# The slots' bias as a one-row product in TensorE, and the last low-rank additions dealt to VectorE and GpSimd in turn

## What is computed

```python
query = hidden_states @ Wq.T
rq = query @ Wr.T
rk = aux_keys @ Wr.T
router_scores = jnp.einsum('bsr,nr->bsn', rq, rk) / np.sqrt(RDIM) + log_rel
top_scores, top_idx = jax.lax.top_k(router_scores, K)
sel_keys = aux_keys[top_idx]
attn = jnp.einsum('bsd,bskd->bsk', query, sel_keys) / np.sqrt(BOT) + log_rel[top_idx]
w = jax.nn.softmax(attn, axis=-1)
...
aux_out = aux_out @ Wvd.T @ Wvu.T
...
gate = jax.nn.sigmoid(gate_w1 * u_norm + gate_bias)
...
return hidden_states + gate[..., None] * aux_out
```

## Time and profile before

| | us |
|---|---|
| median of 3 runs | 1425.62 (1423.89 to 1426.12) |
| the profiled execution | 1426.41 |
| its span, first to last instruction | 1423.6 |
| PE busy | 1351.8 (95%) |
| DVE busy | 1177.8 (83%) |
| ACT busy | 953.3 (67%) |
| POOL busy | 704.9 (50%) |

### The profile page before, as it was taken

One profiled execution on the slowest core, in us unless ns is written; L12 is line 12 of the kernel. 1 busy time (PEld: TensorE's weight loads), 2 busy tenths in 40 slices (PEclk: granted clock), 3 DMA queues, 4 the chain that ended last, 5 costly groups with the idle time before them and its releaser, 6 DMA issues.

```text
span 1423.6 us, 25847 instructions
## 1 busy us (share of the span) xinstructions
PE 1351.8 (95%) x8474; PEld 754.3 (53%) x8604; DVE 1177.8 (83%) x2877; ACT 953.3 (67%) x2463; POOL 704.9 (50%) x596
## 2 busy tenths in 40 slices
PE   4779999998999999999999999999999999999995
PEld 3444555554455555555555555555555555555553
DVE  7887978889899887988878898889777798778657
ACT  5568777676677676667667667667666676666754
POOL 3376767677765344445545454435543454434321
PEclk8899999999999999999999999999999999999998
DMA  8466766787777566656567655657666677556443
GB/s 281 164 137 136 199 184 174 186 190 176 179 167 167 109 146 147 138 126 146 140 127 165 134 132 141 127 127 161 135 138 124 141 147 160 113 136 134 93 89 119
DMA packets 439828, 211.20 MB, mean 148 GB/s; under 512 B 382016, under 2 KB 383344, under 8 KB 439696
## 3 DMA queue, kind: packets, MB, share of 16 engines
q1 hardware_dynamic: 438144, 208.18, 63.6%
q10 hardware_dynamic: 1552, 1.38, 0.3%
HBM read 91.00 MB, written 25.17 MB: 82 GB/s over the span
## 4 chain that ended last, share of the span: by engine, by line
PE 70%; DVE 15%; ACT 5%; issue 4%; POOL 4%; DMA 1%; DVEq 0%; SPq 0%; ACTq 0%
PE PJ L1536 16%; PE PJ L1537 15%; PE PJ L1535 15%; DVE phl L1256 4%; PE PV L1708 4%; PE PV L1703 4%; PE PV L1704 4%; PE SC L1724 4%; PE SC L1722 4%; PE SC L1723 4%; POOL t L629 2%; ACT p L839 2%; DVE p L1246 2%; DVE t L1202 2%; DVE t L1200 1%
## 5 line engine op out<-in xcount | busy, mean ns | idle before, releaser
L651 POOL TENSOR_TENSOR oTl<-of,oTf 128x512 f16<-128x512 f32 x128 | 154.1, 1204 | 437.3 <-ACT oTf L831 437.1
L839 ACT ACTIVATE p<-p,mn 128x512 f32<-128x512 f32 (+3 forms) x512 | 280.9, 550 | 96.6 <-DVE mn L1246 96.5
L1256 DVE SCALAR_TENSOR_TENSOR phl<-p,ri,phl 128x128 f16<-128x128 f32 (+3 forms) x512 | 329.3, 683 | 0.0
L850 ACT ACTIVATE phl<-p,ri 128x128 f16<-128x128 f32 (+3 forms) x512 | 245.6, 550 | 4.1
L1535 PE MATMUL PJ<-XT,wsp 128*128 128x512 f16 x628 | 238.9, 380 | 4.0 <-DVE t L1202 3.9
L629 POOL TENSOR_TENSOR t<-t 128x512 f32<-128x512 f32 x158 | 201.7, 1277 | 77.3 <-DVE t L1202 76.8
L1536 PE MATMUL PJ<-XT,wsp 128*128 128x512 f16 x628 | 238.8, 380 | 0.0
L1537 PE MATMUL PJ<-XT,wsp 128*128 128x512 f16 x628 | 238.5, 380 | 0.0
L1246 DVE CUSTOM_DVE_ANT_0 p<-SC,maskw 128x512 f32<-128x512 f32 (+3 forms) x512 | 219.8, 485 | 2.1
L1536 PE MATMUL PJ<-wosp,oTf 128*128 128x512 f16 x512 | 194.0, 379 | 4.3
L634 POOL TENSOR_TENSOR qTl<-t,qTh 128x512 f16<-128x512 f32 x127 | 148.5, 1170 | 92.5 <-ACT qTh L815 92.5
(11 more groups left out here) (263 smaller groups left out, 2589.6 us busy)
## 6 DMA issues: line engine op xcount, KB each, us to landing
wsp<-kept SPq DMA_DIRECT2D x146, 256.0 KB, 3.0
wosp<-kept SPq DMA_DIRECT2D x96, 256.0 KB, 3.2
raw<-in_wqkv SPq DMA_DIRECT2D x48, 256.0 KB, 3.5
kept<-wsp SPq DMA_DIRECT2D x42, 256.0 KB, 2.5
raw<-in_wo SPq DMA_DIRECT2D x32, 256.0 KB, 4.4
kept<-wosp SPq DMA_DIRECT2D x32, 256.0 KB, 3.0
pTf<-phl SPq DMA_TRANSPOSE x256, 3.8
X<-in_x SPq DMA_DIRECT2D x3, 1024.0 KB, 9.8
```

The lines of the kernel that those rows point to most:

```text
L839: ins = nc.scalar.activation(pt, pt, ACT.Exp, bias=mn[:, par, i:i + 1], scale=-1.0, accum_out=rs[:, par, i:i + 1])
L850: nc.scalar.activation(phl[:, par, high(i, 0):high(i, i) + 1:3, :], p[:, par, SOFF[i]:SOFF[i] + w].rearrange("p (k t) -> p k t", t=P), ACT ...
L1256: nc.vector.scalar_tensor_tensor(out=phl[:, par, low(i, 0):low(i, i) + 1, :], in0=p[:, par, SOFF[i]:SOFF[i] + w].rearrange("p (k t) -> p k ...
```

## The change

For the two batches that are done apart (the first FFN's first, the second FFN's last), the bias goes into PSUM by PE: a product with one row (`ones[0:1]` by `lr2`, f32, 256 columns) starts each of the four score tiles, and the three 16-bit products add to it. `lr2` holds the bias and its negative. The factors go into `bh` and `bl` when they are made (`fqb`). `take_scores` is left out there, and `top` reads the scores from PSUM. In the other batches `take_scores` stays, with a plain addition.

`query_factors` in the head gets two factors more and, behind a wait for `ld_fs`, the two instructions that fill `lr2`.

At the end tiles 7, 9 and 11 go the way of 1, 3 and 5: scaled by ACT, added by POOL. POOL's first addition waits until the last selection is done (`r_mn[1]`). DVE's additions 0 and 2 stand behind `inverse_sums`, 4 and 6 behind `e_lo`. The products are made in the order 5, 7, 4, ET, 6, 8, 9, 11, 10, 12 to 15. The variance of tiles 14 and 15 is made behind the norming of tile 12 and ahead of that of tile 13.

```diff
-        + [(("AUX", 1, 1, n - 4), n) for n in (4, 5, 6)] + [(("ET", 1, 3, 0), 1)]
-        + [(("AUX", 1, n // 4, n % 4), k) for n, k in ((7, 7), (8, 3), (9, 0), (10, 2), (11, 4), (12, 5), (13, 6), (14, 7),
-                                                       (15, 3))])
+        + [(("AUX", 1, n // 4, n % 4), k) for n, k in ((5, 5), (7, 7), (4, 4))] + [(("ET", 1, 3, 0), 1)]
+        + [(("AUX", 1, n // 4, n % 4), k) for n, k in ((6, 6), (8, 0), (9, 3), (11, 5), (10, 2), (12, 4), (13, 7), (14, 6),
+                                                       (15, 0))])
...
-        odd = [1, 3, 5]
+        odd = [1, 3, 5, 7, 9, 11]
...
+            pool.wait_ge(r_mn[1], NT)
             for n in odd:
                 aux_add(n)
...
             exps_ffn(1, bb, (3,))
+            aux_odd(5)
             tail_sigmoid(10, 12, NT)
             e_hi(1, bb)
-            aux_odd(5)
+            aux_odd(7)
             tail_sigmoid(11, 12, NT)
             base(2, bb, 3)
+            aux_odd(9)
+            aux_odd(11)
...
-                nc.vector.scalar_tensor_tensor(out=rsc[:, ts, :], in0=both[:, :, 0:NSLOT], scalar=RDIM ** -0.5, in1=lr,
-                                               op0=ALU.mult, op1=ALU.add)
...
+                nc.vector.tensor_tensor(rsc[:, ts, :], both[:, :, 0:NSLOT], lr, ALU.add)
...
             def top(f, bb, tiles):
-                dve.wait_ge(r_use[f], 4 * bb + tiles[-1] + 1)
+                if apart(f, bb):
+                    dve.wait_ge(r_sc[f], 4 * bb + tiles[-1] + 1)
+                    if bb:
+                        dve.wait_ge(r_t[f], 4 * bb)
+                    route = {i: score_bank(f, bb, i)[:, 0:NSLOT] for i in tiles}
+                    attn = {i: score_bank(f, bb, i)[:, NSLOT:2 * NSLOT] for i in tiles}
...
                 nc.vector.reciprocal(fqr[:, :], fqs[:, :]).then_inc(fs_dve, 1)
+                nc.vector.tensor_scalar(fqb[:, 0:1], fqs[:, :], RDIM ** -0.5, None, ALU.mult)
+                nc.vector.tensor_scalar(fqb[:, 1:2], fqs[:, :], -BOT ** -0.5, None, ALU.mult).then_inc(fs_dve, 1)
+                dve.wait_ge(ld_fs, 96)
+                nc.vector.tensor_copy(lr2[0:1, 0:NSLOT], lrb[0:1, :])
+                nc.vector.tensor_scalar(lr2[0:1, NSLOT:2 * NSLOT], lrb[0:1, :], -1.0, None, ALU.mult).then_inc(fs_dve, 1)
...
             def select_first(i):
-                take_scores(0, 0, (i,))
                 top(0, 0, (i,))
...
             normal(2, bb, 0)
+            variance_of_squares(2, 4)
             normal(2, bb, 1)
-            variance_of_squares(2, 4)
...
             def select(*tiles):
-                take_scores(1, bb, tiles)
                 top(1, bb, tiles)
...
-            add(0)
-            add(2)
             learned(1, bb)
             gate_1(1, 12, NT, 4)
             inverse_sums(1, 12, NT, 4)
-            add(4)
-            add(6)
+            add(0)
+            add(2)
             dve.wait_ge(g_exd, 11)
             gate_2(1, 12, NT)
             e_lo(1, bb)
-            add(7)
+            add(4)
+            add(6)
             dve.wait_ge(g_exd, 12)
             gate_3(12, NT)
             scales(1, 12, NT)
-            for n in range(8, NT):
+            add(8)
+            add(10)
+            for n in range(12, NT):
                 add(n)
...
+                    if apart(f, bb):
+                        mm(dst, ones[0:1, :], lr2[:, :], start=True, stop=False)
+                    mm3(dst, qfh[:, ts], qfl[:, ts], bh[:, :], bl[:, :], not apart(f, bb), True).then_inc(r_sc[f], 1)
```

More of the change, by code:

```diff
@@ L145 @@
 PREPARED = {"pe": ["rk", "rmat", "wqT", "u1T", "v2"], "act": ["rk", "wq sums", "wq rows", "wq", "b0", "b1", "wu1", "v2"],
-            "dve": ["wq scales", "wq", "b0", "b1", "u1T", "v2"]}
+            "dve": ["wq scales", "b scales", "lr2", "wq", "b0", "b1", "u1T", "v2"]}
 def prepared(engine, what):
@@ L249, in macaron_kernel @@
         fql, fqs, fqr = (sb(n, [P, 1], F32) for n in ("fql", "fqs", "fqr"))
+        fqb = sb("fqb", [P, 2], F32)
+        lr2 = sb("lr2", [1, 2 * NSLOT], F32)
         fwvdT = sb("fwvdT", [P, CC, VB], F32)
@@ L356, in rope_index, with product @@
             return 5 * n if kind == "K" else 5 * n + idx + 1
-        odd = [1, 3, 5]
+        odd = [1, 3, 5, 7, 9, 11]
+        PRODUCTS = [4 * t[2] + t[3] for t, _ in TAIL if t[0] == "AUX"]
+        def product(f, n):
+            return PRODUCTS.index(n) + 1 if f else n + 1
         def odd_tile(f, n):
@@ L888, in _ @@
             act.wait_ge(fs_pe, prepared("pe", "rmat"))
-            nc.scalar.activation(bh[:, 0:NSLOT], SC[:, 1, 0:NSLOT], ACT.Copy, scale=fqs[:, 0:1]).then_inc(fs_act, 1)
-            nc.scalar.activation(bh[:, NSLOT:2 * NSLOT], fkeyT[:, :], ACT.Copy, scale=fqs[:, 0:1]).then_inc(fs_act, 1)
+            act.wait_ge(fs_dve, prepared("dve", "b scales"))
+            nc.scalar.activation(bh[:, 0:NSLOT], SC[:, 1, 0:NSLOT], ACT.Copy, scale=fqb[:, 0:1]).then_inc(fs_act, 1)
+            nc.scalar.activation(bh[:, NSLOT:2 * NSLOT], fkeyT[:, :], ACT.Copy, scale=fqb[:, 1:2]).then_inc(fs_act, 1)
             act.wait_ge(ld_fu, 16)
@@ L983, in aux_odd @@
             def aux_odd(n):
-                act.wait_ge(r_aux[1], n + 1)
+                act.wait_ge(r_aux[1], product(1, n))
                 act.wait_ge(r_gs[1], 1 if n < 12 else 2)
@@ L1079, in take_scores @@
                 i0, i1 = tiles[0], tiles[-1] + 1
-                if len(tiles) == 2:
-                    both = bank(("SCR", f, bb, i0 // 2)).rearrange("p (t n) -> p t n", t=2)
-                else:
-                    both = score_bank(f, bb, i0).unsqueeze(1)
+                both = bank(("SCR", f, bb, i0 // 2)).rearrange("p (t n) -> p t n", t=2)
                 lr = lrb[:, :].unsqueeze(1).to_broadcast([P, i1 - i0, NSLOT])
@@ L1101, in top @@
             def top(f, bb, tiles):
-                dve.wait_ge(r_use[f], 4 * bb + tiles[-1] + 1)
+                if apart(f, bb):
[4 more added lines that the diff above has]
+                    attn = {i: score_bank(f, bb, i)[:, NSLOT:2 * NSLOT] for i in tiles}
+                else:
+                    dve.wait_ge(r_use[f], taken(f, bb) + tiles[-1] + 1)
+                    route = {i: rsc[:, i, :] for i in tiles}
+                    attn = {i: asc[:, f, i, :] for i in tiles}
                 for i in tiles:
-                    ins = nc.vector.max(m8[:, i, :], rsc[:, i, :])
+                    ins = nc.vector.max(m8[:, i, :], route[i])
                 link(ins)
                 for i in tiles:
-                    ins = nc.vector.match_replace(mr[:, i, :], m8[:, i, :], rsc[:, i, :], SELECTED)
+                    ins = nc.vector.match_replace(mr[:, i, :], m8[:, i, :], route[i], SELECTED)
                 link(ins)
@@ L1182, in aux_add @@
                 n = 4 * bb + i
-                dve.wait_ge(r_aux[f], n + 1)
+                dve.wait_ge(r_aux[f], product(f, n))
                 dve.wait_ge(x_up[2 * f], n + 1)
```

20 lines of the change are left out of this document (11 added, 9 removed).

## The result

The changed kernel takes 1434.0 us (median of 6 runs, 1432.04 to 1434.97) against 1425.87 us for the kernel before in the same session: a ratio of 1.0057, 95% interval 1.0046 to 1.0068. It is 8.1 us slower. The forecast was 1427.1, and its range ended at 1429.6: the sign was right, the size was not. The profiled execution has a span of 1433.2 us, 9.6 more than before (the two executions themselves, 1434.97 and 1426.41, are 8.56 apart; 1 us of the difference lies outside the spans).

A forecast was written before the change was run, and what follows sets the result against it. PE's chain (70% of the span) was taken to bound the kernel, the output's stores its end. Head +1.7 and end -0.2 gave +1.5 on the median 1425.62: 1427.1 us, range 1424.4 to 1429.6.

The forecast's parts named there:

- The clock in the head and at the end: Head: clock rises when it did, giving back 0.8 us of the query's 1.5 delay; end: low-clock cost kept as before.
- PE stays at its lower clock in the head: Rival, head: PE's standstill during DVE's wait delays the clock's rise, 2.5 us more, 1429.6 us; chance 0.17.
- The one-row product: Both stages: each f32 product of 256 columns takes 0.45 us, bounds 0.22 to 0.56; four add 1.8 us on PE.
- The wait: Head: DVE waits for the constants, norming tiles 2 and 3 3.0 us later; the query starts 1.5 late.
- The copies left out: DVE saves 2.1 us in the head's four tiles, partly lost waiting for u1T; at the end only 0.5 of 1.8 counts.
- DVE idles ahead of `gate_3`: Sign at the end: DVE waits 2.2 us for ACT's sigmoid, as hidden layer and gelu come 0.8 later.
- The third store sets the end: End: the output's stores bound it; third store leaves at 1415.8 behind POOL's additions, so the end gains 0.2 us.
- DVE's last addition: Sign at the end: with three additions fewer (2.0 us) DVE finishes near 1416.9, covered by the output.
- the dealing by itself: End: tiles 7, 9 and 11 go from DVE to ACT and POOL; the end as a whole was forecast to gain 0.2.
- Reading from PSUM: Both stages: selection reading PSUM counted as nothing; the rival that it is dear, 0.8 us a stage, had chance 0.04.
- the sign of the whole: Whole kernel: forecast slower by 1.5 us; chances 0.24 for slower by over 0.2%, 0.70 same, 0.06 faster.

The follow-up runs named there:

- e2: Changed kernel with the f32 bias product made of all 128 rows, bias in every partition, weights 1/128: 1427.73 us, ratio 1.0016.
- e13: Changed kernel with the bias product widened to 128 rows, rows 1 to 127 zero, weights all 1: 1427.63 us, ratio 1.0014.
- e14: As e2, but 32 rows in the f32 bias product, weights 1/32: 1430.02 us, ratio 1.0027.
- e1: Changed kernel with only the filling of lr2 and its wait moved behind the second score weight's low half: 1432.32 us, ratio 1.0042.
- e5: As e2, with lr2 filled later, behind the second score weight's low half: 1427.11 us, ratio 1.0005.
- e9: As e2, but 64 rows in the f32 bias product, weights 1/64: 1430.30 us, ratio 1.0035.
- e6: As e5, but the bias as two f16 products of 128 rows instead of one f32 product: 1425.11 us, ratio 0.9993.

## Why the prediction was wrong, step by step

**The clock in the head and at the end, the step that failed.** The prediction let the clock rise "when it did" (read from the products' steps; the column PEclk doesn't show that rise) and give back 0.8 us of the query, and kept the rest at the higher level. In its place: nothing came back (the query took 3.18, before 3.19; the rise came 2.4 later, as late as the query), and the clock fell in the one-row products, in both stages. The first of the two differs from one execution to the next: from the query's first product to its last it is 2.98 us here and 3.08 before, but 2.43, 2.38 and 2.40 in e2, e13 and e14, with the same PE instructions up to the scores, so some 0.7 did come back there. The second is what cost. By the rows that is 2.37 us in the head's hidden layer (5.05 less 2.68) and 0.7 in the last score tile (1.76 from 23.61 to 25.37, less 1.06), and at the end 1.35 in the hidden layer (3.28 at the gelu less 1.93 at its start); from the end's first product to the gelu's product the changed kernel takes 18.46, e14 with the same emptying and the clock up 16.82, a difference of 1.64. e2 and e14 show that it hangs on the one row. The rival "PE stays at its lower clock in the head" had the right engine and a chance of 0.17, but its cause was DVE's wait, which e1 rules out, its place was the head alone, and its price, 2.5, was some two thirds of what the clock cost there (3.4 to 3.6, below).

**The one-row product, a term that was too small.** 0.45 was taken, with 0.56 as the high bound, from half of a product of 512 columns and 32 rows. The f32 product as such was sized rightly: with 128 rows it adds 0.43 to a tile (0.76 less 0.33). With one row it adds 0.73, outside the bounds, since PE empties around it. In each stage that is 1.2 us more than with 128 rows. The prediction priced the product alone and not what it does to the loads of its neighbours.

**The wait, a term that was too small.** 3.0 us on DVE and 1.5 at the query were forecast; 4.31 and 2.61 came, 1.2 of each because `gb` landed 10.0 us after its issue and not 8.8. The rest is as forecast, 3.1 and 1.4. The landing time of one execution was taken as the time, and it was the shortest of the sixteen on record. What the wait costs in the end, 1.6 to 2.1 by e1 and e5, is less than what it delays.

**What was right, and what looked so.** The copies left out count only in part: the selection's second half in the head starts with `u1T`, which is late. DVE idles ahead of `gate_3`, released by ACT (4.36, forecast 2.2; the gelu is 3.28 late and not 0.8, 1.6 of it by the clock and most of the rest by the emptying). The third store sets the end, 7.68 us behind its issue, and waits for POOL's tile 11, as forecast. DVE's last addition is covered, but it ends at 1426.75, which on the old time base of the end (7.24 less) is 1419.5 and not the 1416.9 given as a sign: it comes later than before the change (1418.55), with 4.36 us of waiting ahead of `gate_3` on its way. That the dealing by itself is worth the forecast 0.2 can't be told from the scatter. Reading from PSUM costs nothing. That the sign of the whole came out right is owed to the head's wait and products; the larger part of the loss was not in the forecast.

**The sum, by stages.** Head: wait 1.8 (e2 less e5), f32 products of 128 rows 1.2 (e5 less before), one row instead of 128 4.4 (changed less e2), together 7.47. To split the last, count from the first bias product to the hand-over, so that the landing of `gb` is left out: 37.11 in the changed kernel, 32.81 in e2, 33.50 in e9, 33.66 in e14. The emptying is 0.7 to 0.9, the clock 3.4 to 3.6. End: one row instead of 128 3.0 (changed less e2), and -0.64 for all the rest of the change, together 2.36; the third store's issue, free of what happens behind it, says the same (32.62 us into the stage, 29.63 in e2, 30.28 before).

## What to carry over

A product with one row among products of 128 is dear in more than its own time: like one with 32 or 64 rows it makes PE run empty on both sides (0.30 us a time here), and with one row it cost the clock of what followed. Padding it to 128 rows with zeros, set once (e13), gave some 6 us back, more than anything else that was tried; two f16 parts in place of the f32 product, with 128 rows, gave 1.7 to 2.0 more (e6). Even so no kernel with the bias in PE in both stages was clearly faster than the one before. Where a kernel's output flows at the rate of its DMAs, look for the stretches in which they stand still and let the stores go in smaller parts, each as soon as its tiles are done.
